# Expert steps of a fused attention and expert kernel: score maxima in pairs of pairs around the outer products, and another split of three PSUM banks

## The reference

```python
h = _layernorm(x) * (1 + ca) + sa
x = x + ga * attention(h)
h = _layernorm(x) * (1 + cb) + sb
x = x + gb * experts(h)
# experts, for t = one token's slice of 32 channels
w = softmax(t @ expert_emb); topw, topi = top_k(w, 2)
hmid = gelu(einsum('td,edi->tei', t, W1) + b1)
eo = einsum('tei,eio->teo', hmid, W2) + b2
comb = (take(eo, topi) * topw).sum(1)
out = comb @ Wo + bo
```

## Time and profile before

| | |
|---|---|
| runs | 2918.32, 2919.54, 2922.02 us |
| median | 2919.54 us |
| the profiled execution: its own time | 2920.5 us |
| its span | 2918.1 us |
| granted TensorE clock, mean | 0.992 |
| PE busy | 2816.6 us (97%) |
| DVE / ACT / POOL busy | 64% / 62% / 43% |

### The profile page before, as it was taken

One profiled execution on the slowest core, in us unless ns is written; L12 is line 12 of the kernel. 1 busy time (PEld: TensorE's weight loads), 2 busy tenths in 40 slices (PEclk: granted clock), 3 DMA queues, 4 the chain that ended last, 5 costly groups with the idle time before them and its releaser, 6 DMA issues.

```text
span 2918.1 us, 50109 instructions
## 1 busy us (share of the span) xinstructions
PE 2816.6 (97%) x16476; PEld 1241.9 (43%) x16476; DVE 1863.0 (64%) x4638; ACT 1808.5 (62%) x2148; POOL 1246.2 (43%) x1325
## 2 busy tenths in 40 slices
PE   7899999999999999999999999999999999999999
PEld 3344444444444443444444444444444444444433
DVE  5775666756666666666667666675756657667553
ACT  2346675566755677457675576655666566665687
POOL 4312645136451364414654146531565215561254
PEclk9899999999999999999999999999999999999999
DMA  6203453044430444304432055311453124530343
GB/s 156 57 5 99 118 130 73 1 108 122 120 71 8 119 118 107 71 21 121 122 97 61 23 134 130 87 47 46 121 133 89 32 71 119 124 88 20 77 127 94
DMA packets 176972, 252.96 MB, mean 87 GB/s; under 512 B 50509, under 2 KB 83293, under 8 KB 176621
## 3 DMA queue, kind: packets, MB, share of 16 engines
q1 hardware_dynamic: 176100, 248.44, 34.3%
q10 hardware_dynamic: 620, 1.34, 0.2%
HBM read 159.13 MB, written 12.63 MB: 59 GB/s over the span
## 4 chain that ended last, share of the span: by engine, by line
PE 86%; DVE 7%; issue 3%; ACT 2%; POOL 1%; SPq 1%; DMA 1%; ACTq 0%; DVEq 0%; POOLq 0%
PE ps L1279 17%; PE ps L1321 17%; PE ps L1339 16%; PE ps L1305 9%; PE ps L428 7%; PE ps L477 4%; PE ps L479 2%; PE ps L518 2%; PE ps L548 2%; DVE rest L573 1%; PE ps L529 1%; PE ps L505 1%; PE ps L536 1%; PE ps L463 1%; PE ps L487 1%
## 5 line engine op out<-in xcount | busy, mean ns | idle before, releaser
L1411 ACT ACTIVATE rest<-ps 128x1024 f32<-128x1024 f32 x1024 | 993.8, 1024 | 341.1 <-PE ps L1321 340.9
L1393 ACT ACTIVATE rest<-ps 128x1024 f32<-128x1024 f32 (+3 forms) x768 | 610.2, 809 | 537.4 <-PE ps L1279 511.6
L1518 POOL TENSOR_TENSOR rest<-rest 128x512 f32<-128x512 f32 x478 | 632.0, 1322 | 560.7 <-DVE rest L1448 548.1
L1448 DVE SCALAR_TENSOR_TENSOR rest<-ps,b2c,wide 128x512 f32<-128x512 f32 x512 | 384.0, 750 | 489.8 <-PE ps L1339 451.7
L1321 PE MATMUL ps<-wide,w1s 98*128 98x512 f32 x2048 | 655.1, 437 | 11.5 <-ACT rest L1411 8.7
L1339 PE MATMUL ps<-rest,w2s 128*32 128x512 f32 x4096 | 546.1, 605 | 0.6 <-ACT rest L1411 0.6
L1508 POOL TENSOR_SCALAR_AFFINE_SELECT rest<-rest 128x256 f32<-128x256 f32 x512 | 206.4, 411 | 772.3 <-ACT rest L1393 770.3
L573 DVE CUSTOM_DVE_ANT_0 rest<-ps,maskd 128x512 f32<-128x512 f32 (+3 forms) x1024 | 444.8, 487 | 118.8 <-PE ps L428 114.0
L1279 PE MATMUL ps<-wide 49*128 49x512 f32 (+3 forms) x2304 | 486.3, 511 | 10.2 <-ACT rest L1393 4.2
L1321 PEld LDWEIGHTS ps<-wide,w1s 98*128 98x128 f32 x2048 | 340.8, 188 | 301.0 <-ACT rest L1411 189.0
L576 DVE TENSOR_REDUCE front<-ps 128x1 f32<-128x512 f32 x512 | 329.0, 684 | 92.9 <-PE ps L428 88.7
(11 more groups left out here) (142 smaller groups left out, 2192.4 us busy)
## 6 DMA issues: line engine op xcount, KB each, us to landing
wide<-gate_rows SPq DMA_DIRECT2D x1024, 128.0 KB, 2.8
wide<-front SPq DMA_DIRECT2D x480, 64.0 KB, 2.0
wide<-front SPq DMA_DIRECT2D x192, 128.0 KB, 2.3
ao<-in_x SPq DMA_DIRECT2D x16, 512.0 KB, 5.1
heads<-front SPq DMA_DIRECT2D x64, 128.0 KB, 2.3
xs<-in_x SPq DMA_DIRECT2D x16, 512.0 KB, 5.0
out<-xs SPq DMA_DIRECT2D x32, 256.0 KB, 2.7
wide<-ao SPq DMA_DIRECT2D x96, 64.0 KB, 2.3
```

Source lines behind the costliest of these rows:

```text
L1393: nc.scalar.activation(L.pt[:, u % PTS, :, f:HALF], L.ps[:, 2 * (u % 2):2 * (u % 2) + 2, 0:HALF - f], ACT.Exp, scale=SCALE).then_inc(S["c_ ...
L1411: nc.scalar.activation(L.hm[:, u % HM, :], bank(2 * (u % 2), 2), ACT.Gelu).then_inc(S["e_gelu"], 1)
L1448: v.scalar_tensor_tensor(out=dst, in0=bank(L2 + q % 2), scalar=L.b2c[:, e:e + 1], in1=L.gb[:, q // 2 % GB, q % 2, :], op0=ALU.add, op1=ALU ...
L1518: g.tensor_tensor(dst, dst, L.gy[:, k % GY, :], ALU.add).then_inc(S["e_add"], 1)
```

## The change

The outer products use bank 4 alone, so `outer(q)` waits for `gated(q-1)`. The side ring gets banks 6, 7 and 5. A step's items come in two lists, ahead of and behind the outer products: PE does them ahead of and behind `outer(q-1)`, DVE ahead of and behind `gated(q-1)`. The 25 pairs stand in 13 steps, every second one from 28 to 54 (36 aside), one ahead and one behind (the last step has one). `rmax` moves from step 53 to 48. All other items stay in their steps, behind.

```diff
@@ expert_slots
-    slots = [[] for _ in range(NQ)]
+    slots = [([], []) for _ in range(NQ)]
     def at(q, *items):
-        slots[q].extend(items)
+        slots[q][1].extend(items)
...
-    steps = [28, 30, 32, 34, 35] + [37, 38, 39, 41, 42, 44, 45, 47, 48, 49, 50, 51, 52] + [53, 55, 57, 59, 60, 61, 62]
-    for q, (g, p) in zip(steps, wanted):
-        at(q, ("pair", g, *p))
+    steps = [28, 30, 32, 34, 38, 40, 42, 44, 46, 48, 50, 52, 54]
+    for n, (g, p) in enumerate(wanted):
+        slots[steps[n // 2]][n % 2].append(("pair", g, *p))
     at(36, ("row", 0, 0))
-    at(53, ("rmax", 0))
+    at(48, ("rmax", 0))
@@ all_images
-        before = {5: ("e_gy", NQ), 6: RE[-1].last(6), 7: RE[-1].last(7)} if img else {b: O.R.last(b) for b in (5, 6, 7)}
+        before = {b: (RE[-1] if img else O.R).last(b) for b in (5, 6, 7)}
...
-        RE.append(Ring([item for slot in eslots[img] for item in slot] + [("out", 2), ("out", 3)] * (img + 1 == B), (6, 7),
+        RE.append(Ring([item for slot in eslots[img] for part in slot for item in part] + [("out", 2), ("out", 3)] * (img + 1 == B), (6, 7, 5),
                        "f_p", {"v": "f_v", "a": "f_a"}, 0, FRONT_MOVED, L.junk_b,
-                       {6: RA[img].last(6), 7: RA[img].last(7)}))
+                       {b: RA[img].last(b) for b in (5, 6, 7)}))
@@ values
-                    pe.wait_ge(S["e_gy"], NQ - 1)
+                    pe.wait_ge(S["e_gy"], NQ)
@@ outer
-                if q >= 2:
-                    pe.wait_ge(S["e_gy"], q - 1)
-                elif q == 1:
-                    name, count = RA[img].last(L2 + 1)
-                    pe.wait_ge(S[name], count)
+                if q:
+                    pe.wait_ge(S["e_gy"], q)
                 else:
                     pe.wait_ge(S["c_o"], len(SEQ))
                 for h in range(4):
-                    mm = pe.matmul(bank(L2 + q % 2)[FD * h:FD * h + FD, :], L.w2s[:, e, :],
+                    mm = pe.matmul(bank(L2)[FD * h:FD * h + FD, :], L.w2s[:, e, :],
@@ tensor, and vector alike with item_vector and gated
+                    ahead, behind = eslots[img][q]
+                    for item in ahead:
+                        item_matmuls(pe, L, RE[img], item)
                     if q:
                         outer(img, q - 1)
-                    for item in eslots[img][q]:
+                    for item in behind:
                         item_matmuls(pe, L, RE[img], item)
```

More of the change, by code:

```diff
@@ L1426, in _ @@
                         outputs(len(SEQ) - 1, NM - 1)
-                    for item in eslots[img][q]:
+                    ahead, behind = eslots[img][q]
+                    for item in ahead + behind:
                         item_scalar(act, nc, L, RE[img], item)
@@ L1447, in gated @@
                     dst = L.gy[:, k % GY, :]
-                v.scalar_tensor_tensor(out=dst, in0=bank(L2 + q % 2), scalar=L.b2c[:, e:e + 1],
+                v.scalar_tensor_tensor(out=dst, in0=bank(L2), scalar=L.b2c[:, e:e + 1],
                                        in1=L.gb[:, q // 2 % GB, q % 2, :], op0=ALU.add,
@@ L1479, in _ @@
                 for q in range(NQ):
+                    ahead, behind = eslots[img][q]
+                    for item in ahead:
+                        item_vector(v, L, RE[img], item)
                     if q:
                         gated(q - 1)
-                    for item in eslots[img][q]:
+                    for item in behind:
                         item_vector(v, L, RE[img], item)
```

## The result

The changed kernel takes 2934.09 us (2930.35 to 2934.94), the kernel before beside it 2919.54 us; the ratio is 1.0047, with a 95% interval of 1.0033 to 1.0062. So it is 0.5% slower, at the time that was forecast. The profiled execution took 2934.09 us with a span of 2932.4 us, 14.3 us more than before, at the same mean granted clock of 0.992.

The account below looks back on a forecast made before the run. Bound: PE's own work plus what holds PE. Seven images at 1.36 us (pair steps) plus 0.42 (front), and 1.8 for the last image, made 14.3 us more: 2934 us, 0.5% slower, range 2922 to 2944 us.

Parts of the forecast that it names:

- Pairs, two and two: Steps 28 to 62 of the seven images with pairs: pairs in every second step cost 1.36 us more per image.
- holds: Inner product after a short unheld step just misses ACT's GELU, losing 0.17 us; 17 per image with pairs against 9.
- rival (a): Pair ahead of the outer products is cheap: 9 us less, 2925 us; chance 0.12.
- The third bank in the pair steps: Second pair of a step finds its ring bank free in time, with 0.06 us or more; costed at nothing.
- Rival (c): Second pair waits for the first's reading: from 0.06 us lateness, each 0.1 us costs 8 us; chance 0.11.
- One bank for the outer products: Waiting for the previous gated reading stays covered, by 0.24 us in steps without a pair, except where DVE is behind.
- Rival (d): Outer products wait for the reading in every step: at the whole 0.75 us, 378 us, 3312 us; chance 0.01.
- Steps 9 to 12: Outer products wait for late DVE: PE comes out 2.44 us late in step 12, step 9's 1.29 us included.
- The ring's waits: Third bank removes four side ring waits, in steps 12, 13 and 25 and at the router's matmuls: 2.02 us together.
- The last image: Without pairs or next layernorm: waits of 1.29 us for `xn` and 0.51 us in step 16, so 1.8 us.
- (b): Inner products in the pair steps: ACT gains enough lead that no step is held; 2914 us, or 2911; chance 0.07.
- (e): Front nets a gain and pair steps are held less often than counted; the parts cancel, 2921 us; chance 0.11.

Follow-up runs that it names:

- the short GELU: Kernel before and changed kernel, each with GELU computing 960 of a unit's 1024 columns: 2909.0 us (ratio 0.9968) and 2919.84 us (ratio 1.0006).
- the consecutive pairs: Kernel before with its own banks, one pair behind in every step 28 to 35 and 37 to 53, rmax at 47: 2913.33 us, ratio 0.9986.
- `xn` out of POOL's way: Changed kernel with POOL's addition of step 5 ahead of the power and that of step 7 waiting for `xn`: 2922.93 us, ratio 1.0017.
- the ring of two: Changed kernel with only banks 6 and 7 for the side ring, bank 5 idle: 3000.82 us, ratio 1.0279.
- the split `xn`: Changed kernel with the second half of `xn` moved from step 7 to step 8, behind gated: 2946.07 us, ratio 1.0089.
- the addition of step 5 moved: Changed kernel with POOL's addition of step 5 put ahead of the power for that step's statistics: 2929.4 us, ratio 1.0032.

## Why the prediction was right

- **Pairs, two and two (1.36 us forecast, 1.62 measured).** The count of holds was right: each even step from 30 to 54, and behind it the worth of four. That they are ACT's, the short GELU shows; that they follow a short step, the consecutive pairs show. The pair ahead was taken at its upper bound, 0.44 us, and costs 0.43; rival (a), the cheap pair, is out. Of the 0.26 us over the forecast some 0.12 are the four small waits for the second pair's bank. Divided by what PE works on, the 1.62 are 1.43 from inner products, 0.14 from outer products (these waits) and 0.06 from pairs; the inner products so grew by 0.07 more than 8 x 0.17, and that, with the pairs' 0.06, I could not place.
- **The third bank in the pair steps (0 forecast).** It fits. The margin was smaller than written, because a release by DVE takes 0.14 us here and not the 0.05 of ACT, and the first head takes 0.78 us to read, not 0.70, when it is masked in two parts. Rival (c) happened in four steps of twelve by 0.03 us each, 0.12 us an image or 0.8 in all, a tenth of the 8 us that it was priced at. Without the bank the cost is 7.7 us an image.
- **One bank for the outer products.** In steps without items it stays covered, as the row said: PE has no idle time ahead of the outer products at 731.58. Rival (d) is out, and with it the rule of the Trainium skill (Perfetto Trace Analysis, Matmuls) as a reason against this half; it does bite in steps 9 to 12, where the reader is late (1.31, 0.85 and 0.16 us), and at the last image's last outer products (0.97 us).
- **Steps 9 to 12 (2.44 us forecast).** 1.39 in step 9, 0.93 in step 11 and 0.16 in step 12 make 2.48. The size was right, and so was the step it rests on, that PE's delay does not delay DVE: the readings of steps 9 and 12 are as late against the start of their image as before. (DVE does not go "without a rest", though: it waits 1.10 us for POOL's `rstd` ahead of `norm_rows`, in both kernels alike.) But one would conclude too much from it. The text ahead let PE's wait in step 9 be a part of what it owes in step 12, as if an earlier DVE paid back all of it. With `xn` out of POOL's way DVE does rest, 0.24 us at 640.92, for want of outer products, and step 11's wait stays at 0.86. Only 1.35 of the 2.48 us hang on `xn`; the rest has work of its own ahead of it.
- **The ring's waits (2.02 us forecast).** 0.52 in step 12, 0.94 in step 13, 0.74 in step 25, and 0.10 in step 18, which I had missed: 2.30 us. By these terms the front nets 0.18 us, by the stretch 0.22, instead of 0.42.
- **The last image (1.8 us forecast, 1.99 and 0.41 measured).** The term left out is the last outer products, which have no inner product ahead of them and so wait for the whole reading. Step 17's wait was left out as well. The lower clock in the profiled execution before hid these 0.4 us and gave 1.1 on top.
- **The sum.** 14.3 us forecast, 14.3 between the spans, 14.5 between the medians. The agreement is better than the terms deserve: +1.8 us in the pair steps, -1.4 in the front, +0.5 in the attention slots (the part of a hold in step 63), +0.2 in the last image, -1.1 at the end. That they cancel is luck. The 1.48 us that the last matmuls gained (5.17 to 3.69) are not the change's; without them the spans would differ by 15.8 us, an estimate from these rows.
- **Rivals (b) and (e)** are out: the holds became more and not fewer, and the front lost.
- **The expectations.** The kernels that undid or moved a part came within 4 us. Four did not: the two with the short GELU (I counted a whole hold of 0.17 us as gone where 0.12 went), the ring of two (each second pair waited 0.54 us or more where I wrote 0.5, and step 28 lost 1.30) and the split `xn`, where I took the instruction's mean as its price.

## What to carry to other kernels

Count the steps in which a handshake is just missed, not only the work: moving work that was there anyway made 17 holds of 9, and putting it into consecutive steps made 4. Before a buffer is given from one user to another, look for the few steps in which its reader is late; here giving it over only behind those steps turned a loss of 0.15% into a gain of 0.4%. And before an instruction is moved, look at the spread of its single durations and at what runs on the neighbouring engine in the long ones.

## What the runs showed of the hardware

- A `TENSOR_SCALAR` of 128x256 from SBUF to SBUF takes 0.40 us on DVE alone and up to 1.51 beside a POOL addition of 1.28; the readings out of PSUM (L1448) take 0.74 to 0.75 us either way, and the statistics (L299), from SBUF to SBUF, 0.40 to 0.41.
- A hold of PE is more than its wait. PE misses the GELU by 0.07 us and loses 0.17, since the weights are then loaded in the open; a GELU 0.05 us shorter gives back 0.12 of it.
- PE starts 0.05 us after the end of an ACT row that releases it, and 0.14 to 0.15 us after DVE's (642.23 to 642.37 here, 640.30 to 640.45 with the addition of step 5 moved).
